# A recurrent graph network: 512-wide sums and differences moved from GpSimd to VectorE

## What is computed

```
x = layernorm(x + L0(x))     # y = (adj x + x) W + b, rows scaled to length 1
x = layernorm(x + L1(x))     # 5 steps of a gated recurrent unit over the graph:
                             #   m = adj h ; z, r = sigmoid(...m, h...) ; c = tanh(...m, r*h...)
                             #   h = (1 - z) h + z c
x = layernorm(x + L2(x))     # symmetric-normalised adj, then W and b
x = layernorm(x + L3(x))     # softmax attention over edges, own part apart, then bias
```

## Time and profile before

| | TensorE | VectorE | ScalarE | GpSimd |
|---|---|---|---|---|
| busy, us | 771.1 | 706.7 | 557.4 | 336.2 |
| share of the span | 94% | 86% | 68% | 41% |

### The profile page before, as it was taken

How to read it: one execution, slowest core, us unless ns; L and a number is a source line. 1 busy time by engine, 2 the same in 40 slices (tenths; PEclk the granted TensorE clock), 3 DMA queues, 4 the chain that set the end, 5 groups by cost and what they waited for, 6 DMA issues and landing times.

```text
span 820.2 us, 12050 instructions
## 1 busy us (share of the span) xinstructions
PE 771.1 (94%) x3646; PEld 628.4 (77%) x3648; DVE 706.7 (86%) x1494; ACT 557.4 (68%) x1118; POOL 336.2 (41%) x269
## 2 busy tenths in 40 slices
PE   7899978789999999999999999999988899999994
PEld 6677756677888888888888888878876777888883
DVE  4679999989988888888888888888999999888776
ACT  4688866668666666666666666656676777788777
POOL 2677655544322222222222222232345575645333
PEclk9999999999999999999999999999999999999998
DMA  6200000010100000000000000000000000000112
GB/s 213 82 2 0 1 1 0 1 52 1 52 1 1 1 1 1 1 0 0 0 0 1 0 0 0 0 1 1 1 1 1 2 0 2 1 1 1 52 52 103
DMA packets 8794, 12.98 MB, mean 16 GB/s; under 512 B 2721, under 2 KB 3873, under 8 KB 8481
## 3 DMA queue, kind: packets, MB, share of 16 engines
q1 hardware_dynamic: 8736, 12.33, 4.4%
HBM read 7.09 MB, written 5.24 MB: 15 GB/s over the span
## 4 chain that ended last, share of the span: by engine, by line
PE 66%; DVE 26%; ACT 3%; issue 2%; POOL 1%; DMA 1%; SPq 0%; ACTq 0%
PE agg_ps L920 10%; PE agg_ps L922 10%; PE agg_ps L921 10%; PE gate_ps L883 6%; PE gate_ps L885 6%; PE gate_ps L884 6%; DVE feat_lo L767 5%; DVE reset_lo L776 4%; PE cand_ps L883 3%; PE cand_ps L885 3%; PE cand_ps L884 3%; PE turn_ps L980 3%; DVE stats L791 3%; DVE cand L754 2%; DVE agg_lo L749 2%; DVE res L743 2%
## 5 line engine op out<-in xcount | busy, mean ns | idle before, releaser
L579 POOL TENSOR_TENSOR feat<-feat,cand 128x512 f32<-128x512 f32 x80 | 135.3, 1691 | 323.8 <-DVE cand L758 323.8
L429 ACT ACTIVATE agg_hi<-agg_ps 128x512 fp32r<-128x512 f32 x128 | 76.2, 596 | 120.3 <-PE agg_ps L922 120.0
L920 PE MATMUL agg_ps<-adj_hi,nat_hi 128*128 128x512 f32 x384 | 151.9, 396 | 0.0
L922 PE MATMUL agg_ps<-adj_hi,nat_lo 128*128 128x512 f32 x384 | 150.1, 391 | 0.0
L921 PE MATMUL agg_ps<-adj_lo,nat_hi 128*128 128x512 f32 x384 | 149.6, 390 | 0.0
L749 DVE TENSOR_TENSOR agg_lo<-agg_ps,agg_hi 128x512 fp32r<-128x512 f32 x128 | 88.0, 688 | 71.2 <-ACT agg_hi L429 71.0
L767 DVE TENSOR_TENSOR feat_lo<-feat,feat_hi 128x512 fp32r<-128x512 f32 x80 | 140.7, 1759 | 0.0
L606 POOL TENSOR_TENSOR rstd<-mean_var,half 128x4 f32<-128x4 f32 x64 | 71.1, 1111 | 115.2 <-DVE mean_var L798 115.0
L883 PE MATMUL gate_ps<-agg_hi,w_hi 128*128 128x512 f32 x208 | 89.5, 431 | 5.1 <-DVE agg_lo L749 4.6
L390 ACT ACTIVATE res<-res,shift,rstd 128x128 f32<-128x128 f32 x214 | 92.3, 484 | 1.6 <-DVE shift L807 1.5
L449 ACT ACTIVATE gate_r<-gate_ps,bias 128x512 f32<-128x512 f32 x80 | 55.1, 689 | 47.8 <-PE gate_ps L885 47.8
(11 more groups left out here) (168 smaller groups left out, 1698.0 us busy)
## 6 DMA issues: line engine op xcount, KB each, us to landing
res<-in_x SPq DMA_DIRECT2D x16, 256.0 KB, 5.5
out<-res SPq DMA_DIRECT2D x16, 256.0 KB, 2.0
rows<-in_adj SPq DMA_DIRECT2D x4, 256.0 KB, 4.0
mix_rows<-feat SPq DMA_DIRECT2D x1, 1024.0 KB, 3.9
later<-mix_rows SPq DMA_DIRECT2D x1, 1024.0 KB, 5.0
gate_z<-in_L_gnn_w_w SPq DMA_DIRECT2D x3, 128.0 KB, 4.4
cand<-in_L_gnn_W SPq DMA_DIRECT2D x2, 64.0 KB, 4.1
gate_z<-in_L_gnn_u_w SPq DMA_DIRECT2D x2, 64.0 KB, 4.2
```

The costliest lines, as they stand in the source:

```text
L429: act.activation(agg_hi[:, s % 2, :], agg_ps[s % 2][:, :], ACT.Copy).then_inc(agg_hi_made, 1)
L579: pool.tensor_tensor(feat[:, u % B, :], feat[:, u % B, :], cand[:, u % 2, :], ALU.add).then_inc(state_made, 1)
L920: pe.matmul(ps, nat_hi[:, b, k, :], m_hi[:, k, :], start=(k == 0), stop=False)
L922: last = pe.matmul(ps, nat_lo[:, b, k, :], m_hi[:, k, :], start=False, stop=(k == T - 1))
```

## The change

Three kinds of operation leave GpSimd for VectorE, with the same operands. The low parts of all inputs: that of graph 2 before slot 0, those of 3 to 15 in slots 0 to 12, behind the statistics of the slot; one semaphore counts them. The state's sum: directly behind the product `cand * z`, with a wait for it, ahead of `gate_r * feat`. The splits' `nat_lo`: directly behind the statistics of the slot. GpSimd keeps the powers, the weights' sums, the work on `later` and the constants.

```diff
--- before.py
+++ after.py
@@ -279,7 +279,7 @@
         max_made, exp_made, mix_made = sem("max_made"), sem("exp_made"), sem("mix_made")
         count_made, diag_apart, diag_in, diag_m_made = sem("count_made"), sem("diag_apart"), sem("diag_in"), sem("diag_m_made")
         mix_stored, mix_loaded = sem("mix_stored"), sem("mix_loaded")
-        x_hi_made, x_lo_first, x_lo_rest = sem("x_hi_made"), sem("x_lo_first"), sem("x_lo_rest")
+        x_hi_made, x_lo_made = sem("x_hi_made"), sem("x_lo_made")
         agg_done, agg_hi_made, agg_lo_made = sem("agg_done"), sem("agg_hi_made"), sem("agg_lo_made")
         gate_done = sem("gate_done")
         z_done, cand_done = sem("z_done"), sem("cand_done")
@@ -565,21 +565,7 @@
             pool.iota(kcol_int[:, :], [[1, 1]], base=1, channel_multiplier=1).then_inc(const_made, 1)
             pool.wait_ge(const_made, consts)
 
-            def x_lo(b):
-                pool.wait_ge(x_hi_made, b + 1)
-                pool.tensor_tensor(nat_lo[:, b, :, :], res[:, b, :, :], nat_hi[:, b, :, :].bitcast(F32),
-                                   ALU.subtract).then_inc(x_lo_rest, 1)
-
-            x_lo(2)
-
             def slot(s, ahead):
-                u = s - 2
-                if is_step(u):
-                    pool.wait_ge(move_made, ahead(u - B + 1))
-                    pool.tensor_tensor(feat[:, u % B, :], feat[:, u % B, :], cand[:, u % 2, :],
-                                       ALU.add).then_inc(state_made, 1)
-                if s + 3 < B:
-                    x_lo(s + 3)
                 if s == 2:
 
                     pool.wait_ge(param_in, PARAMS)
@@ -588,11 +574,6 @@
                     for i, a, b in ((B_R, 1, 3), (B_Z, 0, 3), (B_H, 2, 4)):
                         pool.tensor_tensor(bias[:, i:i + 1], bias_raw[:, a:a + 1], bias_raw[:, b:b + 1], ALU.add)
                     pool.tensor_tensor(folded[:, 1, :], folded[:, 1, :], folded[:, 0, :], ALU.subtract).then_inc(folded_made, 1)
-                for n in norms_at(s, "split"):
-                    if stage(n) != L3:
-                        pool.wait_ge(split_hi_made, nth(SPLIT, n))
-                        pool.tensor_tensor(nat_lo[:, n % B, :, :], res[:, n % B, :, :],
-                                           nat_hi[:, n % B, :, :].bitcast(F32), ALU.subtract).then_inc(split_lo_made, 1)
                 for n in norms_at(s, "turn"):
                     if stage(n) == L0:
                         r = length[:, n % 4, :]
@@ -640,7 +621,7 @@
             def x_lo(b):
                 dve.wait_ge(x_hi_made, b + 1)
                 dve.tensor_tensor(nat_lo[:, b, :, :], res[:, b, :, :], nat_hi[:, b, :, :].bitcast(F32),
-                                  ALU.subtract).then_inc(x_lo_first, 1)
+                                  ALU.subtract).then_inc(x_lo_made, 1)
 
             for t in range(T):
                 dve.wait_ge(adj_in[t], 16)
@@ -655,6 +636,7 @@
             dve.tensor_tensor(w_lo[:, W_L0:W_L3 + 1, :], cand[:, 0, 0:2 * D].rearrange("p (a d) -> p a d", d=D),
                               w_hi[:, W_L0:W_L3 + 1, :].bitcast(F32), ALU.subtract).then_inc(w0_lo_made, 1)
             x_lo(1)
+            x_lo(2)
 
             def slot(s, ahead):
                 def turn_of(*key):
@@ -757,6 +739,9 @@
                     dve.wait_ge(z_made, ahead(u - B + 1))
                     dve.tensor_tensor(cand[:, u % 2, :], cand[:, u % 2, :], gate_z[:, u % 2, :],
                                       ALU.mult).then_inc(move_made, 1)
+                    dve.wait_ge(move_made, ahead(u - B + 1))
+                    dve.tensor_tensor(feat[:, u % B, :], feat[:, u % B, :], cand[:, u % 2, :],
+                                      ALU.add).then_inc(state_made, 1)
                 u = s - 1
                 if is_step(u):
                     dve.wait_ge(r_made, ahead(u - B + 1))
@@ -797,6 +782,13 @@
                     dve.wait_ge(aggregated, i + 1)
                     dve.tensor_scalar(mean_var[:, i % RING, :, 1], mean_var[:, i % RING, :, 1], EPS_LN, None,
                                       ALU.add).then_inc(stats_made, 1)
+                for n in norms_at(s, "split"):
+                    if stage(n) != L3:
+                        dve.wait_ge(split_hi_made, nth(SPLIT, n))
+                        dve.tensor_tensor(nat_lo[:, n % B, :, :], res[:, n % B, :, :],
+                                          nat_hi[:, n % B, :, :].bitcast(F32), ALU.subtract).then_inc(split_lo_made, 1)
+                if s + 3 < B:
+                    x_lo(s + 3)
                 if UNITS - B <= s < UNITS:
                     dve.wait_ge(self_hi_made, s - (UNITS - B) + 1)
                     dve.tensor_tensor(self_lo[:, :], feat[:, s % B, :], self_hi[:, :].bitcast(F32),
@@ -896,10 +888,7 @@
 
                 if s < UNITS:
                     if s < B:
-                        if s < 2:
-                            pe.wait_ge(x_lo_first, s + 1)
-                        else:
-                            pe.wait_ge(x_lo_rest, s - 1)
+                        pe.wait_ge(x_lo_made, s + 1)
                     elif 2 * B <= s < AFTER:
                         pe.wait_ge(turn_read, ahead(reads(TURN_NO["state", s - B])))
                     else:
```

## The result

The changed kernel takes **806.6 us** (median of 4 runs, 806.03 to 807.19) against 819.21 us (4 runs) for the kernel before; the ratio of the runs is 0.9846, 95% interval 0.9826 to 0.9865. The forecast was 806.0, in a range of 799 to 815. The profiled execution spans 804.8 us, 15.4 less than before's 820.2. In every run that has both numbers the device time lies 1.6 to 1.8 us above the span (806.6 and 804.8 here), so before's profiled execution, put down as an ordinary run, took an estimated 822 us, more than any timed run of that kernel (up to 821.06).

The account below looks back on a forecast made before the run. TensorE was taken to bound slots 31 to 79, VectorE slots 18 to 24 and 89 to 96, slowed by GpSimd collisions. Terms from -5.4 to +1.0 summed to -13.9, from 820.2 to 806 us; range 799 to 815.

Parts of the forecast that it names:

- the two slower ones: Rivals: reset_lo too late in slots 31 to 79, 831 us, chance 0.05; feat_lo's 1.79 us not GpSimd's doing, 845, 0.03.
- Slots 89 to 96: -5.4: VectorE-bound slots: sum, feat_lo, reset_lo and nat_lo terms take each slot from 7.99 to 7.32 us, -5.4.
- Slots 18 to 24: -4.7: VectorE-bound slots: the same four terms, -0.67 per slot, 9.29 to 8.6 us, -4.7 over seven.
- the `later` products "at zero": Slots 18 to 24: GpSimd's four products may collide elsewhere, +0.4 to -0.6 in each of some six slots, taken at zero.
- the third rival: Smaller gain: collisions move onto other two-input or two-port operations and slots 5 to 15 become VectorE's; 815 us, chance 0.14.
- Slots 0 to 4: -1.0: VectorE's wait for a GpSimd power goes, 0.6 left after added work; half-clock stretch may go too, 1.6; estimate -1.0.
- Slots 25 to 30: -1.8: VectorE falls below TensorE, which sets the time; -2.5 without the clock's fall, -0.9 with it, estimate -1.8.
- Slots 31 to 79: 0: TensorE-bound slots of 6.60 us: no change if reset_lo comes in time.
- the forecast's slack: Slots 31 to 79: reset_lo would end 0.65 us before TensorE loads for it.
- Slots 80 and 81: -0.5: affine_select leaves these slots, -1.3, and runs soon after slot 30, where 0.8 was set aside; -0.5.
- The small terms: Slots 16 and 17 -1.2, slots 5 to 15 -0.3, slots 97 to 104 +1.0, after slot 105 zero.
- a power that holds nat_lo: Norms' slots: by the lock rule a GpSimd power would hold a nat_lo starting behind it for its whole length.

Follow-up runs that it names:

- the kernel with the fills: The changed kernel plus three GpSimd fills of a 128x512 tile, reading nothing, in slots 88 to 97: 807.66 us.
- the sum behind feat_lo: The changed kernel with the state's sum on VectorE moved from ahead of gate_r to behind feat_lo: 799.71 us.
- the split alone: The kernel before with only the low part of the normed rows (split's nat_lo) moved to VectorE: 810.99 us.
- the kernel with the operations placed: The changed kernel with GpSimd's remaining 512-wide `later` operations issued ahead of the power, waiting for the previous unit's reset_lo: 799.94 us.
- inputs alone: The kernel before with only the low parts of the inputs moved to VectorE: 814.2 us.
- state's sum alone: The kernel before with only the state's sum moved to VectorE: 816.5 us.
- GpSimd's added sum: The changed kernel plus one 512-wide GpSimd sum per slot in slots 88 to 97, its result unread: 816.83 us.

## Why the prediction was right, and where it was not

**The mechanism.** The sum rested on one claim: a 512-wide GpSimd operation lengthens a VectorE operation with two SBUF inputs by 1.1 us. That is shown, by taking it away (feat_lo 1.79 to 0.69) and by putting it back where nothing depends on it (+1.10 per slot). The 1.1 us are not a fixed price, though (last section): they hold where VectorE's operation starts 0.5 us behind GpSimd's. Of the rivals, the two slower ones did not occur: TensorE's matmuls waited nowhere for reset_lo between 206 and 531 us, a weight load once for 0.2, and the time there grew only in slot 31 and at the back-edges.

**Slots 89 to 96: -5.4, measured -5.4.** 7.31 us each for 7.32. The terms, too, are as told: reset_lo starts 0.78 us after feat_lo (612.43 and 611.65 above, in the kernel with the fills, whose slots take the same 7.31), 0.60 and a wait of 0.18, forecast as 0.20.

**Slots 18 to 24: -4.7, measured -1.0. This is the step that failed**, the one that took the `later` products "at zero" within +0.4 and -0.6. Slots 20 to 24 took 9.61 us before; -0.67 gives 8.94, and the measured 9.44 is 0.5 more. The product went from cand's difference (0.54 too long) to the norm pair (1.03 too long), which is that 0.5. The text named the norm's tensor_scalar as a place where it might fall and bounded the cost almost rightly, but took zero; this was the third rival, in this stretch alone. Over slots 20 to 24 this is 2.5 of the 3.7 us missing. The text also gave every slot of the stretch the same -0.67, and slot 18 is the other 1.4 us: it took 7.19 us before and 7.92 after, though 7.20 with the sum behind feat_lo: there the sum's 0.73 ahead of gate_r was paid and nothing came back. Slot 19 gave 0.1 more than forecast.

**Slots 0 to 4: -1.0, measured -4.0.** Two things were undersized. Before's stretch at a granted clock of 0.53, near 1.2 GHz, behind TensorE's wait of 2.07 us:

```profile
35.20:38.60 3.40, 3.40 (x13) 2.91 (x14) 2.83 (x8) 1.76 (x7) 0.61 (x1) 0.53 0.01 2
```

After, TensorE waits 0.3 us instead of 2.07 and the granted clock stays at 1.00 between 33 and 38 us. The kernel with the split alone kept the wait and, in its one profiled execution, the full clock: slot 4 took 8.26 in before, 6.67 there and 4.91 after. So 1.6 of the 4.0 us are the clock and 1.8 the wait, which the forecast had at 0.6 net of VectorE's added work; the other 0.6 lie in slots 2 and 3. The added work is paid for: before, GpSimd's low parts of the inputs lengthened several operations of VectorE's there, for example the scan, 5.5 us then and 4.4 after. In all seven profiled kernels that have this part of the change slot 4 took 4.9 to 5.1 us at the full clock; of the three without it two took 8.26 at a clock of 0.79 and one, the split alone, 6.67 at the full one. So the 1.6 is a gain in some executions only.

**Slots 25 to 30: -1.8, measured -2.7**, but for other reasons than the forecast gave. The clock fell here too, about 2 us earlier against the slots (slot 25 begins at 163.6):

```profile
161.50:165.00 3.50, 3.35 (x8) 2.68 (x9) 2.66 (x8) 3.26 (x7) 0.00 (x0) 0.52 0.00 0
```

More than half of that lies in slot 24, which VectorE bounds anyway, and the rest cost nothing: slot 25 took 7.36 us here and 7.35 in the kernel with the operations placed, whose clock stayed at 1.00. Before, the fall lay in slot 25 and cost about 1.3 us over the stretch (inputs alone, above). So of the 2.7 us about half is the clock, although it fell, and half the work. Against this gain stands a loss that the forecast did not see: the sum makes slots 25 to 28 0.7 us longer each than with the split alone (7.98 and 7.97 for 7.24 and 7.25 in slots 26 and 27), and behind feat_lo it does not. So the place of the sum on VectorE sets the time there, and not, as the forecast had it, TensorE's work alone. That it does so through gate_r and reset_hi, as at the back-edges, is likely but not shown: TensorE reads as busy for the whole of these slots in either kernel.

**Slots 31 to 79: 0, measured +0.8.** 6.59 to 6.62 us per slot, with the forecast's slack. But the pairs of slots around the loop's back-edges, 47 and 48, 63 and 64, take 13.5 and 13.6 us where they took 13.2: ScalarE stands 1.68 us in "issue" before gate_z there, in before as well, and reset_hi now ends 0.7 later ahead of it.

**Slots 80 and 81: -0.5, measured -1.3.** affine_select runs at 206.33, at the end of slot 30 as told, and cost nearly nothing there, where 0.8 had been set aside:

```profile
206.33 1.92 POOL L604 TENSOR_SCALAR_AFFINE_SELECT later<-later 128x2048 f32<-128x2048 f32 x1 [49.46 <-DMA later<-mix_rows]
207.09 0.69 DVE L731 TENSOR_TENSOR agg_lo<-agg_ps,agg_hi 128x512 fp32r<-128x512 f32 x1 [0.33 <-ACT agg_hi L429]
207.93 0.86 DVE L736 TENSOR_TENSOR cand<-cand,feat 128x512 f32<-128x512 f32 x1 [0.15 <-ACT cand L435]
```

It fell on an operation with a PSUM input and only touched the next (0.86 for 0.69).

**The small terms.** Slots 16 and 17: -1.1 for -1.2; 5 to 15: -0.7 for -0.3; 97 to 104: +1.2 for +1.0; after 105: +0.3 for nothing. All came from the parts to which they were put down: the split, the inputs, and sum and split together.

**The total** is right because the errors cancel: +3.7 in slots 18 to 24, -3.0 in slots 0 to 4, -0.9 and -0.8 in 25 to 30 and at 80, +0.8 in the loop. The span fell by 15.4, of which 1.8 lie ahead of slot 0. The forecast also took the span of 820.2 and the median of 820.14 for the same base, while the profiled execution was an estimated 1.9 us slower than that median (1.8 us between span and device time); the -13.9 read from it met a fall of the medians of 12.6, from a base of 819.21. The mechanism earned the forecast, the total was luckier than its terms.

Open is what makes the clock fall in one execution and not in another: no experiment held it fixed.

## What to carry to other kernels

Before judging VectorE full, look for its operations with two SBUF inputs that take 1.7 us for 0.68, and for what GpSimd reads at that moment: work moved to the full engine can cost less there than beside it. What must stay on GpSimd belongs beside VectorE's PSUM-input work and its statistics, held there by a wait; a moved neighbour shifts it onto something else, so list what lies beside it after the move. And put an added operation behind those that another engine waits for: the same sum cost 0.7 us per slot more ahead of gate_r than behind feat_lo in slots 26 to 28, and 0.3 in slots 91 to 96.

## What the runs showed of the hardware

- VectorE's operation ends a fixed time behind GpSimd's. In the kernel before 105 of its 128x512 operations with two SBUF inputs start while a GpSimd operation of that width or the affine_select runs, and each of them ends 0.53 to 0.56 us after that one (308.58 and 308.03; the earlier trace rows: 148.14 and 147.60; the earlier trace rows: 548.60 and 548.06). So the price is what is left of GpSimd's operation less about 0.13 us, from 0.33 to 1.72 us in that trace, and 1.1 is only its commonest size. The 22 operations with a PSUM input that start so took 0.66 to 0.69 us, as elsewhere.
- The collision is not one-sided. GpSimd's power takes 1.01 to 1.02 us where no VectorE operation with two SBUF inputs starts beside it (slots 89 to 96 of the kernel before and of the one with the state's sum alone) and 1.38 behind VectorE's nat_lo, which keeps its 0.68. In slots 21 to 24, where nat_lo is followed by more such work, it took 1.47. The forecast had thought of a power that holds nat_lo; it is the other way round, nat_lo having started 0.17 us earlier (135.18 and 135.35 above). GpSimd's added sum, too, took 1.80 us behind VectorE's where the one beside a PSUM-input operation took 1.30.
- Three GpSimd fills of a 128x512 tile, 1.70 us in all, lengthened none of the VectorE operations beside them.
- A pair of 128x128 tensor_scalar operations with one tensor input collides as well: 1.63 us for 0.60 beside a GpSimd product.
- GpSimd's nat_lo took 1.73 us before, where it started at 616.58 while VectorE's feat_lo ran until 617.17, and 1.28 in the kernel with the sum alone, where it started beside a PSUM-input operation. In each of these pairs it is the operation that starts second that is lengthened.
